# Layer 0 of a compressed interaction network: each matmul cut into two halves of 64 output columns, the second half one step behind

## The reference, cut to what matters

```
z = einsum('bmd,bhd->bdmh', x, prev).reshape(b, D, m * h)
t = einsum('bdc,co->bdo', z, ws[k]) + bs[k]
t = transpose(t, (0, 2, 1))
t = t / sqrt(sum(t * t, axis=(-2, -1)))
```

## Time and profile before

| | us |
|---|---|
| median of 3 runs | 1302.21 (1300.32 to 1302.42) |
| span of the profiled execution, first to last instruction | 1297.4 |
| TensorE busy | 1217.8 (94%) |
| VectorE busy | 904.4 (70%) |
| ScalarE busy | 78.1 (6%) |
| GpSimd busy | 205.2 (16%) |
| mean granted TensorE clock | 0.991 of full |

### The profile page before, as it was taken

How to read it: one execution, slowest core, us unless ns; L and a number is a source line. 1 busy time by engine, 2 the same in 40 slices (tenths; PEclk the granted TensorE clock), 3 DMA queues, 4 the chain that set the end, 5 groups by cost and what they waited for, 6 DMA issues and landing times.

```text
span 1297.4 us, 9951 instructions
## 1 busy us (share of the span) xinstructions
PE 1217.8 (94%) x2868; PEld 538.6 (42%) x2868; DVE 904.4 (70%) x898; ACT 78.1 (6%) x155; POOL 205.2 (16%) x245
## 2 busy tenths in 40 slices
PE   0599999999999999999999999999999999999898
PEld 0244444444444444444444444444444444444343
DVE  0468877777787777778777777887777788777640
ACT  0100000000000000000000000000000000000001
POOL 5554654546440000000000000000000000000000
PEclk9899999999999999999999999999999999999998
DMA  7938356290935528092653809165380917444010
GB/s 221 361 58 314 75 195 194 70 316 12 325 63 202 170 87 285 0 323 49 219 153 107 265 0 332 39 233 138 121 250 9 330 32 254 118 145 170 1 41 0
DMA packets 58974, 203.70 MB, mean 157 GB/s; under 512 B 11131, under 2 KB 14331, under 8 KB 58966
## 3 DMA queue, kind: packets, MB, share of 16 engines
q1 hardware_dynamic: 47478, 195.26, 46.1%
q0 software_dynamic: 7424, 3.19, 1.8%
q10 hardware_dynamic: 4064, 5.15, 1.2%
HBM read 201.67 MB, written 1.90 MB: 157 GB/s over the span
## 4 chain that ended last, share of the span: by engine, by line
PE 91%; DVE 4%; issue 2%; DMA 2%; ACT 1%; POOL 1%; SPq 0%; POOLq 0%; ACTq 0%
PE acc L405 83%; PE acc L392 5%; DVE z L308 2%; PE acc L453 1%; DMA xr<-xt 1%; PE nrm L414 1%; POOL gathered L154 1%; PE t_ps L459 1%; DVE inv L328 1%; DMA gathered<-in_table,rows_of 0%; PE acc L454 0%; ACT root L250 0%; DVE prod L330 0%; DVE rnorm L335 0%; DVE half L332 0%
## 5 line engine op out<-in xcount | busy, mean ns | idle before, releaser
L405 PE MATMUL acc<-z,w_sb 128*128 128x512 f32 x2496 | 1087.4, 596 | 27.4 <-DVE z L308 27.4
L308 DVE TENSOR_TENSOR z<-t_ps,xb 128x1536 f32<-128x1536 f32 x416 | 711.9, 1751 | 186.0 <-PE acc L405 185.6
L405 PEld LDWEIGHTS acc<-z,w_sb 128*128 128x128 f32 x2496 | 472.4, 191 | 617.7 <-issue 545.8
L154 POOL DMA_INDIRECT gathered<-in_table,rows_of x160 | 154.3, 964 | 57.6 <-issue 43.9
L392 PE MATMUL acc<-z,w_sb 117*128 117x512 f32 (+1 forms) x224 | 104.4, 609 | 40.7 <-DVE z L295 40.7
L316 DVE TENSOR_REDUCE ssum<-sq 128x32 f32<-128x512 f32 x48 | 32.6, 679 | 111.6 <-ACT traw L245 111.6
L295 DVE TENSOR_TENSOR z<-x,xr 117x512 f32<-117x512 f32 (+1 forms) x112 | 68.8, 682 | 29.5 <-DMA xr<-xt 29.5
L243 ACT ACTIVATE sq<-acc,bias 128x512 f32<-128x512 f32 x48 | 33.0, 687 | 808.8 <-PE acc L405 771.8
L392 PEld LDWEIGHTS acc<-z,w_sb 117*128 117x128 f32 (+1 forms) x224 | 42.1, 194 | 88.1 <-issue 87.1
L162 POOL DMA_DIRECT2D xt<-gathered x32 | 29.8, 932 | 76.9 <-DMA gathered<-in_table,rows_of 74.4
L245 ACT ACTIVATE traw<-acc,bias 128x512 f32<-128x512 f32 x48 | 32.7, 681 | 0.0
(11 more groups left out here) (23 smaller groups left out, 51.1 us busy)
## 6 DMA issues: line engine op xcount, KB each, us to landing
xb<-xt SPq DMA_DIRECT2D x208, 768.0 KB, 6.4
xr<-xt SPq DMA_DIRECT2D x48, 468.0 KB
x<-xt SPq DMA_DIRECT2D x48, 78.0 KB
gathered<-in_table,rows_of POOLq DMA_INDIRECT x160
xr<-xt SPq DMA_DIRECT2D x32, 78.0 KB
xt<-gathered POOLq DMA_DIRECT2D x16, 72.0 KB, 2.9
xb<-in_wt SPq DMA_DIRECT2D x1, 768.0 KB, 4.6
xt<-gathered POOLq DMA_DIRECT2D x32, 6.0 KB, 2.1
```

What stands on the lines that cost most here:

```text
L154: nc.gpsimd.indirect_dma_start(gathered[0:n, g, :], None, table[:, :], bass.IndirectOffsetOnAxis(rows_of[0:n, g:g + 1], 0)).then_inc(rows_ ...
L308: nc.vector.tensor_tensor(z[:, s % ZSLOTS, :, :], fields_of(k, c), xb[:, c * CH:(c + 1) * CH, :], ALU.mult).then_inc(z_ready, 1)
L405: last = nc.tensor.matmul(acc[k][:, :], w_sb[k][:, m, :], z[:, s % ZSLOTS, r, :], start=(m == 0), stop=(m == FIELDS - 1))
```

## The change

Line 392's matmul of 128 output columns becomes two of 64. The first, `half0(k)`, writes partitions 0 to 63 of `acc[0]`; the second, `half1(k)`, writes partitions 64 to 127 and is issued one step later, behind `half0(k + 1)`. Both read all of the step's products. After the last step one `half1` follows by itself and increments `acc0_ready`.

```diff
+            HALF = UNITS // 2
+
             def layer0(i, parts):
                 for k in parts:
                     if k == 0 and not (isinstance(i, int) and i == 0):
                         pe.wait_ge(raw_ready[0], 2 * i)
-                    n = WIDE if k < STEPS0 - 1 else NARROW
                     pe.wait_ge(z0_ready, STEPS0 * i + k + 1)
-                    last = nc.tensor.matmul(acc[0][:, :], w0_sb[0:n, k, :], z0[0:n, k, :],
-                                            start=(k == 0), stop=(k == STEPS0 - 1))
+                    half0(k)
+                    if k > 0:
+                        half1(k - 1)
                 if parts[-1] == STEPS0 - 1:
-                    last.then_inc(acc0_ready, 1)
+                    half1(STEPS0 - 1).then_inc(acc0_ready, 1)
+
+            def half0(k):
+                n = WIDE if k < STEPS0 - 1 else NARROW
+                return nc.tensor.matmul(acc[0][0:HALF, :], w0_sb[0:n, k, 0:HALF], z0[0:n, k, :],
+                                        start=(k == 0), stop=(k == STEPS0 - 1))
+
+            def half1(k):
+                n = WIDE if k < STEPS0 - 1 else NARROW
+                return nc.tensor.matmul(acc[0][HALF:P, :], w0_sb[0:n, k, HALF:UNITS], z0[0:n, k, :],
+                                        start=(k == 0), stop=(k == STEPS0 - 1))
```

## The result

The changed kernel takes 1305.27 us (median of 18 runs, 1301.61 to 1309.26) against 1301.18 us before (18 runs, 1298.57 to 1303.00): ratio 1.0034, 95% interval 1.0026 to 1.0043. It is slower by 4 us, where 24 were forecast. The interval of the difference is 3.4 to 5.6 us.

What follows compares the result with a forecast made beforehand. TensorE, 94% busy, was taken as the bound, with a wait for VectorE's products at layer 2's start. +0.99 and +0.48 over 15 tiles (22.0 us) plus 1.9 for tile 0 made +23.9: 1326 us, range 1309 to 1392.

Steps and rivals of the forecast that it cites:

- Do two halves run at once?: Layer 0: only neighbouring matmuls of different halves overlap, so 9 slots (3.87 us) on each side of layer 1's norm.
- no visible effect: Rival: overlap, no price for the shape, the added slot before the norm hidden; within 0.2% (2.6 us), chance 0.03.
- The weights in the open: Weight loads showing where layer 0's halves alternate: 0.035 us at each of five neighbours, 0.18 per part.
- +0.99: Layer 0's steps 0 to 3, before the norm: 4.43 us instead of 3.44 in each tile.
- The +1.9 for tile 0: Layer 0 of tile 0: 17 slots instead of 14, a change of shape and loads, 1.9 us more.
- The part behind the norm: Norm and steps 4 to 6: 4.59 us against the 4.11 of VectorE's chain, cover gone, +0.48 per tile.
- up to 1.37 us fit there: Steps 4 to 6, under VectorE's chain: lengthening them costs nothing until they take about 1.37 us more.
- The price of a change of shape: Into and out of both parts of layer 0: 0.19 us each, four per tile, 0.76 us, two before the norm.
- The price of one instruction: Layer 0's matmuls of 64 columns: 0.43 us each, the same as for 128 columns or one.
- Serial: Rival: layer 0's halves go one after another, 5.41 us more per tile, 1378 to 1391 us; chance 0.29.
- Loads in the open at each neighbour: Rival: halves overlap but each neighbour in layer 0 shows its load, 0.14 us; 1343 us, chance 0.1.
- A half below 0.43: Rival: a 64-column matmul of layer 0 costs less, break-even 0.34 us; at half price 1285 us; chance 0.03.

## Why the prediction was wrong

The sign was right, and so was the stretch ahead of the norm as a place where it costs. The size was not: 1.47 us a turn were forecast and 0.34 came, and the 0.48 of it that was to stand behind the norm is not there at all. The range began at 1309 and the time is 1305.27. Of the signs that it named for being right, two came: 448 instructions, and pairs that start within 0.1 us. The others did not: the stretch ahead of the norm is 3.58 and not 4.2 to 4.6, the chain still enters layer 2 through line 308, each tile keeps its wait there, and the turn is 75.55 and not 76.7.

**The step that failed** is the count of slots under "Do two halves run at once?". It granted that different halves overlap, but kept them in the order of the program, so that only neighbours could overlap and the pair h0 h0 at the head cost a slot. The low end of the range and the dismissal of "no visible effect" rest on that slot as well; no rival let a half pass the other. The runs show two streams that do. Even tile 0 shows it, where `half1(0)` starts ahead of the second instruction of `half0(0)`:

```profile
42.25 1.09 PE L403 MATMUL acc<-z,w_sb 117*64 117x512 f32 x1 [42.25 <-DVE z L295]
42.77 1.12 PE L408 MATMUL acc<-z,w_sb 117*64 117x512 f32 x1
43.13 1.06 PE L403 MATMUL acc<-z,w_sb 117*64 117x512 f32 x1
```

The Trainium skill, "TensorE: Matmul & The Clock Gate", Part 3, holds that matmuls start and end in the order of the program. These rows, and the norm's second half in the experiment with the norm in halves, start out of it, so here the measurement decides. What stayed in order was the increment that ScalarE waits for.

With two streams the part ahead of the norm has the 8 slots it had: 3.44 and not 3.87, -0.43. The weights in the open, 0.18, are not there either: in pairs 0.01 to 0.06 apart each half's load lies under its own stream. Of +0.99 so 0.38 is left, the two changes of shape, measured 0.33 to 0.34. This one term carries the sign of the forecast. The +1.9 for tile 0 is not there: from layer 0's first matmul to the norm it takes 11.55 us (42.25 to 53.80) instead of 11.85. That difference prices nothing, since both stretches begin with matmuls 0.85 apart, and the changed kernel has fewer of these.

**The part behind the norm**, forecast at 4.59 and 0.48 over its cover, has 8 slots too: 0.34 from the norm's start to the first matmul (626.84) and 3.49 to the end of the last slot (630.33), 3.83 in all, under the 4.38 that VectorE needs from the same start (4.27 before, 4.11 as the prediction's chain counts). Its price, 0, is shown by the kernel with halves only behind the norm (0.9998). The statement that up to 1.37 us fit there held as far as it was drawn on: the idle time ahead of layer 2 fell from 1.30 to 0.38 us in the changed kernel, and to 0.38 in the one with four steps of halves behind the norm.

**The price of a change of shape**, 0.19 from the tail, nearly held: 0.14 on the way in and 0.19 on the way out, of which 0.10 falls between the norm and ScalarE, where the prediction had nothing. The Trainium skill, "TensorEngine Tiling (Array Packing)", section Tiling Modes, says that changing the mode drains the engine; the trace agrees that a change costs time, 0.34 us for two, and the norm in halves took one of them back. Whether the engine is emptied, no row shows.

**The price of one instruction**, 0.43 whatever the width, held at 64 and at 32 columns.

**Rivals.** Serial was off: it is what the same columns give, 5.30 us ahead of the norm for 12 instructions. Loads in the open at each neighbour: not seen. A half below 0.43: not seen. "No visible effect" was ruled out with the slot of 0.43 as its reason, which is the step that failed; the true cost, 0.34%, is just above the 0.2% that it took as the least that can be told, through the shape alone.

**Two readings of the rows** were off without touching the failed step. The 17 waits of the earlier trace rows are 15 of 1.30 us and two of 4.0, one at the start and one in the last tile, and not 16 of 1.4 to 1.5. And the 4.8 us added to the span is the median of three runs less the span of one execution; the 18 runs of the changed kernel lie 1.6 to 1.7 us above their own spans, those of the kernel before mostly 1.6 to 2.0 and at most 2.9. Its median over 18 runs is 1301.18 and not 1302.21, so 1 us of the 21 between 1326 and 1305 is the base and not the change.

What stays open: what holds a stream back while more than three earlier instructions have not started, and how much of a change of shape is the load in the open.

## What to carry to other kernels

Cutting a full-width matmul into column groups gains nothing in slots, because the full one already fills all columns; what it costs is the change of shape on the way in and out, so either all matmuls of a stretch have the same shape or none is cut. Cut throughout, it gave 0.30 us a turn back here, beside short matmuls. When counting matmuls of different column groups, count each group's stream by itself and take the longest, as long as the groups alternate closely in the program: in these traces no matmul started with more than three earlier ones still to start. Look first at which side of a chained wait an instruction stands: moving one step of layer 0 from ahead of the norm to behind it was worth 15 us, more than three times what the halves cost.

## What the runs showed of the hardware

- Matmuls of different column groups pass each other: a stream 0.8 us ahead of the other (625.79 against 624.99), two or four streams at 0.43 us an instruction each, from the same rows and with loads of their own. At most three earlier instructions were passed, and a stream that was free at 625.24 went on only at 625.80, when three were left.
- The increment of a matmul that ran early was not acted on until 0.31 us after the start of the earlier one in the program.
- A short matmul (32 moving columns) exposes the weight loads beside it; in halves of 64 this costs about 0.10 us less each time where TensorE is what the tile waits for, and 0.30 a tile with what the norm of layer 1 and layer 2's first matmul add.
- A change of shape costs 0.14 us into halves and 0.19 out of them, and 0.27 for both around a norm whose loads stood in the open before.
- 448 or 896 instead of 224 matmul instructions, or 5684 instead of 2868 in all, did not slow TensorE: the turns are 75.55, 75.54 and 74.91.
